# The join between a selective scan with FFN and a mixture-of-experts stage: who makes the last products, x2 and x3

## The reference

```
x1 = x  + tanh(g_xattn[0]) * channel_attention(layernorm(x), ctx)
x2 = x1 + tanh(g_ffn[0])   * ffn(layernorm(x1))
x3 = x2 + tanh(g_xattn[1]) * ssm(ctx, z=layernorm(x2))
out = x3 + tanh(g_ffn[1])  * moe(layernorm(x3))

def ffn(x):                       # ternary weights, groups of 64
    gate, up = split(x @ Wgu.T)   # hidden width 1024
    h = silu(gate) * up
    return rms_norm(h) @ Wp.T

def ssm(ctx, z):                  # 256 channels, 16 states each
    state = state * exp(delta * A) + (delta * u) * B     # along 256 positions
    y = sum over states(state * C) + D * u
    return y * silu(z)

def moe(x):                       # 64 experts, top 8, capacity 128
    probs = softmax(x @ router)
    out[token] += weight * expert(x[token])              # for the 8 chosen
```

## Time and profile before

| | |
|---|---|
| median of three runs | 451.32 us |
| the runs | 449.02 to 453.57 us |
| the profiled execution | 454.34 us |
| its span | 452.6 us |
| busy: PE, DVE, POOL, ACT | 347.7, 323.4, 297.1, 240.5 us |
| mean granted clock of PE | 0.907 |
| transfers | 81.56 MB, mean 180 GB/s |

### The profile page before, as it was taken

How to read it: one execution, slowest core, us unless ns; L and a number is a source line. 1 busy time by engine, 2 the same in 40 slices (tenths; PEclk the granted TensorE clock), 3 DMA queues, 4 the chain that set the end, 5 groups by cost and what they waited for, 6 DMA issues and landing times.

```text
span 452.6 us, 6836 instructions
## 1 busy us (share of the span) xinstructions
PE 347.7 (77%) x1843; PEld 240.3 (53%) x1843; DVE 323.4 (71%) x748; ACT 240.5 (53%) x467; POOL 297.1 (66%) x231
## 2 busy tenths in 40 slices
PE   4838934689897999998990479888888888898860
PEld 2423722245453445454790367767766666776650
DVE  3999598889998998999969845544544444454454
ACT  0999968688897878894438013322332232232210
POOL 3200036698997998998614547888788888888750
PEclk9987875599999989999996569999999899999995
DMA  9910402569979998986002237988888888865557
GB/s 247 376 39 13 140 0 76 178 207 322 275 263 314 277 299 271 302 272 198 0 2 88 90 84 193 224 204 204 202 198 197 197 197 197 199 150 95 85 94 242
DMA packets 62809, 81.56 MB, mean 180 GB/s; under 512 B 6130, under 2 KB 42786, under 8 KB 62786
## 3 DMA queue, kind: packets, MB, share of 16 engines
q1 hardware_dynamic: 51632, 64.43, 45.1%
q0 software_dynamic: 9984, 16.78, 19.3%
q10 hardware_dynamic: 1170, 0.08, 0.3%
HBM read 70.13 MB, written 11.14 MB: 180 GB/s over the span
## 4 chain that ended last, share of the span: by engine, by line
POOL 28%; PE 22%; issue 15%; DVE 12%; ACT 11%; DMA 11%; SPq 0%; DVEq 0%; POOLq 0%
POOL sums L650 9%; POOL ssm L575 7%; POOL ssm L639 6%; DMA ssm<-routed,idx 5%; PE bank L1263 3%; PE bank L1105 3%; PE bank L1051 3%; POOL ffn L594 2%; DMA ssm<-bc_rows 2%; DVE ssm L1470 2%; PE bank L1078 2%; PE bank L1228 2%; PE bank L1241 2%; DMA du<-sums 2%; DVE bank L1465 1%
## 5 line engine op out<-in xcount | busy, mean ns | idle before, releaser
L650 POOL DMA_INDIRECT sums<-ssm,idx x48 | 79.1, 1648 | 19.3 <-issue 13.2
L1588 DVE COPY ssm<-bank 128x256 f32<-128x256 f32 x64 | 27.0, 422 | 79.9 <-PE bank L1228 79.8
L575 POOL TENSOR_TENSOR ssm<-ssm,bc_buf 128x1024 f32<-128x1024 f32 (+1 forms) x33 | 75.9, 2301 | 11.1 <-DMA bc_buf<-bc_rows 3.9
L639 POOL DMA_INDIRECT ssm<-routed,idx x64 | 66.1, 1032 | 25.1 <-issue 16.8
L1470 DVE TENSOR_TENSOR_SCAN ssm<-ssm,bank 128x512 f32<-128x512 f32 x64 | 78.1, 1221 | 5.6 <-issue 2.7
L1263 PE MATMUL bank<-arena,ssm 128*128 (+1 forms) x256 | 56.9, 347 | 2.4 <-DVE ssm L1680 1.8
L918 ACT ACTIVATE ssm<-bank 128x256 f32<-128x256 f32 x64 | 24.5, 383 | 60.8 <-PE bank L1241 59.8
L1051 PE MATMUL bank<-ssm,ident 128*128 128x512 f32 x98 | 49.7, 618 | 8.5 <-POOL ssm L575 6.2
L925 ACT ACTIVATE ssm<-bank 128x96 f32<-128x96 f32 x64 | 16.0, 250 | 71.5 <-PE bank L1263 71.5
L1105 PE MATMUL bank<-xs,wguT 128*128 128x512 bf16 x192 | 46.6, 395 | 7.3 <-POOL xs L561 5.4
L1247 PE MATMUL bank<-ssm,xin 128*128 128x256 bf16 x384 | 52.0, 274 | 0.1
(11 more groups left out here) (219 smaller groups left out, 684.9 us busy)
## 6 DMA issues: line engine op xcount, KB each, us to landing
bc_buf<-bc_rows SPq DMA_DIRECT2D x32, 512.0 KB, 4.4
ssm<-bc_rows SPq DMA_DIRECT2D x22, 512.0 KB, 5.4
arena<-in_L_ffn_gate_proj SPq DMA_DIRECT2D x32, 192.0 KB
arena<-in_L_ffn_up_proj SPq DMA_DIRECT2D x32, 192.0 KB
arena<-in_L_ffn_down_proj SPq DMA_DIRECT2D x32, 192.0 KB
B_last<-bc_rows SPq DMA_DIRECT2D x10, 512.0 KB, 5.4
sums<-zero_f SPq DMA_DIRECT2D x1, 2304.0 KB, 14.1
arena<-in_L_ffn_w_gate_up SPq DMA_DIRECT2D x1, 2048.0 KB, 11.5
```

The source lines that it names most:

```text
L575: pool.tensor_tensor(prod[:, a:b, :], hs[:, a:b, :], C_buf[:, a:b, :], ALU.mult).then_inc(s.prod_ok, 1)
L639: pool.indirect_dma_start(out=xe[:, k, :], out_offset=None, in_=routed, in_offset=bass.IndirectOffsetOnAxis(ap=idx2[:, k, 0:1], axis=0)).t ...
L650: pool.indirect_dma_start(out=sums, out_offset=bass.IndirectOffsetOnAxis(ap=idx2[:, k, 1:2], axis=0), in_=ye[:, k, :], in_offset=None, com ...
```

## The change

Seven edits, all in that stretch.

1. Unit 15's gated product: DVE makes `hidden(15)` behind scan 61, ahead of steps 62 and 63, no longer behind step 63.
2. The last products with C (steps 62 and 63) are one DVE instruction of 128 x 1024 ahead of `coefficient(0)`, no longer two of POOL. PE waits for it with a new semaphore, `last_ok`. POOL makes `add_square(14)` ahead of product 30.
3. PE: `project(15)` comes ahead of `sum_early(15)`, and PE waits for the last scan before it writes the router's mean into bank 6.
4. `keep_projection(1)` is left out: `x2(1)` reads the projection from banks 1 and 2. The logits of the two halves, which go to these banks, wait for `x2` instead.
5. ACT's order: `gate_z(0)`, `keep_y(3)`, `keep_x2(0)`, `gate_z(1)`, `keep_x2(1)`.
6. PE: `own_part` is left out. Both halves' `turn_x2` come first, then the logits of x2 and y2 and `turn_y` of the first half, then those of the second. `turn_y` only transposes y2 into the banks of `x3_of`.
7. DVE adds the turned y2 to x2 in SBUF: `x3(c)`, four instructions behind each `select`, and the statistics read that. ACT makes the routed rows from it, and its four copies of x3 are left out.

```diff
-            def product(q, first=0, steps=2):
+            def product(q):
...
+            add_square(UNITS - 2)
             product(PAIRS - 2)
-            add_square(UNITS - 2)
             add_square(UNITS - 1)
-            product(PAIRS - 1, 0, 1)
-            product(PAIRS - 1, 1, 1)
             rms(1)
...
-            keep_projection(1)
...
+            gate_z(0)
+            keep_y(3)
             keep_x2(0)
-            keep_y(3)
-            gate_z(0)
+            gate_z(1)
             keep_x2(1)
-            gate_z(1)
...
                 for j in range(4 * c, 4 * c + 4):
-                    act.wait_ge(s.x3_ps, j + 1)
-                    act.activation(xn[j], x3_of(j), ACT.Identity, bias=nmr[:, j:j + 1], scale=rstd[:, j:j + 1]).then_inc(s.xn_sb, 1)
-            for q, k in enumerate((5, 4, 0, 3)):
-                act.activation(x_res[:, 2 * q:2 * q + 2, :], bank[k][:, :].rearrange("p (j d) -> p j d", d=D), ACT.Copy).then_inc(s.x3_sb, 1)
+                    act.activation(xn[j], x_res[:, j, :], ACT.Identity, bias=nmr[:, j:j + 1], scale=rstd[:, j:j + 1]).then_inc(s.xn_sb, 1)
...
-                    sum_state(f, 2, s.prod_ok, 2 * f + 2)
-                    sum_state(f, 3, s.prod_ok, 2 * f + 3)
+                    sum_state(f, 2, s.last_ok, 1)
+                    sum_state(f, 3, s.last_ok, 1)
...
-                sum_early(f)
+                if f < UNITS - 1:
+                    sum_early(f)
...
             project(UNITS - 1)
+            sum_early(UNITS - 1)
             squares(1, bank[7])
+            pe.wait_ge(s.scan_ok, STEPS)
...
             def logits_of_x2(c):
 
-                pe.wait_ge(s.po_copy, 4)
+                pe.wait_ge(s.x2_sb, 6 + 2 * c)
...
-            def add_y(c):
-
+            def turn_y(c):
+
+                pe.wait_ge(s.x2_sb, NT)
+                pe.wait_ge(s.y_sb, 4)
                 for j in range(4 * c, 4 * c + 4):
                     for h in halves:
-                        ins = pe.matmul(x3_of(j)[:, h * P:h * P + P], u[:, h, j * P:j * P + P], ident[:, :], start=False, stop=h == 1, skip_group_check=True)
+                        ins = pe.transpose(x3_of(j)[:, h * P:h * P + P], u[:, h, j * P:j * P + P], ident[:, :])
                     ins.then_inc(s.x3_ps, 1)
 
             turn_x2(0)
-            own_part(0)
+            turn_x2(1)
             logits_of_x2(0)
-            turn_x2(1)
-            own_part(1)
+            logits_of_y(0)
+            turn_y(0)
             logits_of_x2(1)
-            logits_of_y(0)
             logits_of_y(1)
-            add_y(0)
-            add_y(1)
+            turn_y(1)
...
             for f in range(UNITS):
-                for k in range(4 * f, 4 * f + 4):
-                    state(k)
-                if f in ON_DVE:
+                state(4 * f)
+                state(4 * f + 1)
+                if f == UNITS - 1:
+                    hidden(f)
+                state(4 * f + 2)
+                state(4 * f + 3)
+                if f in ON_DVE and f < UNITS - 1:
                     hidden(f)
...
-                dve.wait_ge(s.po_copy, 2 * c + 2)
+                if c == 0:
+                    dve.wait_ge(s.po_copy, 2)
+                else:
+                    dve.wait_ge(s.proj_ok, UNITS)
...
-                    dve.scalar_tensor_tensor(out=x_res[:, j, :], in0=xn[j], scalar=coef[:, j:j + 1], in1=x_res[:, j, :], op0=ALU.mult, op1=ALU.add).then_inc(s.x2_sb, 1)
+                    dve.scalar_tensor_tensor(out=x_res[:, j, :], in0=xn[j] if c == 0 else bank[1 + j // 2 - 2][:, (j % 2) * D:(j % 2) * D + D], scalar=coef[:, j:j + 1], in1=x_res[:, j, :], op0=ALU.mult, op1=ALU.add).then_inc(s.x2_sb, 1)
...
+            dve.wait_ge(ld_C[1], 16 * (PAIRS // 2))
+            dve.wait_ge(s.scan_ok, STEPS)
+            dve.wait_ge(s.sum_ok, 3 * (UNITS - 1))
+            dve.tensor_tensor(prod[:, 2:4, :], hs[:, 2:4, :], C_buf[:, 2:4, :], ALU.mult).then_inc(s.last_ok, 1)
             coefficient(0, 1)
             x2(0)
...
+            def x3(c):
+
+                for j in range(4 * c, 4 * c + 4):
+                    dve.wait_ge(s.x3_ps, (j | 1) + 1)
+                    dve.tensor_tensor(x_res[:, j, :], x3_of(j), x_res[:, j, :], ALU.add).then_inc(s.x3_sb, 1)
+
             select(0)
-            half_statistics(4, 0, x3_of, s.x3_ps)
+            x3(0)
+            half_statistics(4, 0, s.x3_sb)
             select(1)
+            x3(1)
             shifts(0)
-            half_statistics(4, 1, x3_of, s.x3_ps)
+            half_statistics(4, 1, s.x3_sb)
```

More of the change, by code:

```diff
@@ L121, in __init__ @@
         self.pair_ok = sem("pair_ok")
+        self.last_ok = sem("last_ok")
         self.hsq_ok = sem("hsq_ok")
@@ L561, in _ @@
                 pool.tensor_tensor(xs[:, 2, kc, c], xnT[:, kc, c], xs[:, 1, kc, c], ALU.subtract).then_inc(s.xs_lo, 1)
-            def product(q, first=0, steps=2):
+            def product(q):
                 pool.wait_ge(ld_C[q % 2], 16 * (q // 2 + 1))
-                pool.wait_ge(s.scan_ok, 2 * q + first + steps)
-                a, b = 2 * (q % 2) + first, 2 * (q % 2) + first + steps
+                pool.wait_ge(s.scan_ok, 2 * q + 2)
+                a, b = 2 * (q % 2), 2 * (q % 2) + 2
                 f = q // 2
@@ L834, in keep_y, with keep_projection @@
                 act.activation(y_buf[:, p % 2, (p // 2) * 512:(p // 2) * 512 + 512], bank[3][:, :], ACT.Copy).then_inc(s.y_sb, 1)
-            def keep_projection(th):
+            def keep_projection():
                 for k in range(2):
-                    act.wait_ge(s.proj_ok, 8 * th + 8)
-                    act.activation(xw[:, 4 * th + 2 * k:4 * th + 2 * k + 2, 0:D], bank[1 + k][:, :].rearrange("p (a m) -> p a m", m=D), ACT.Copy).then_inc(s.po_copy, 1)
+                    act.wait_ge(s.proj_ok, 8)
+                    act.activation(xw[:, 2 * k:2 * k + 2, 0:D], bank[1 + k][:, :].rearrange("p (a m) -> p a m", m=D), ACT.Copy).then_inc(s.po_copy, 1)
             def square(f):
@@ L870, in _ @@
                 if f == 8:
-                    keep_projection(0)
-            keep_projection(1)
+                    keep_projection()
             def keep_x2(c):
@@ L1220, in _ @@
             pe.wait_ge(s.idx_step, 1)
-            pe.wait_ge(s.x3_sb, 4)
+            pe.wait_ge(s.x3_sb, NT)
             pe.sem_inc(s.m_hT_ps, 1)
@@ L1498, in x2, with half_statistics @@
                 for j in range(4 * c, 4 * c + 4):
-                    dve.scalar_tensor_tensor(out=x_res[:, j, :], in0=xn[j], scalar=coef[:, j:j + 1], in1=x_res[:, j, :], op0=ALU.mult, op1=ALU.add).then_inc(s.x2_sb, 1)
-            def half_statistics(n, c, source, ready):
+                    dve.scalar_tensor_tensor(out=x_res[:, j, :], in0=xn[j] if c == 0 else bank[1 + j // 2 - 2][:, (j % 2) * D:(j % 2) * D + D], scalar=coef[:, j:j + 1], in1=x_res[:, j, :], op0=ALU.mult, op1=ALU.add).then_inc(s.x2_sb, 1)
+            def half_statistics(n, c, ready):
                 for j in range(4 * c, 4 * c + 4):
-                    dve.wait_ge(ready, j + 1 if source is x2_of else (j | 1) + 1)
-                    dve.bn_stats(stats[:, j, :], source(j)).then_inc(s.ln_stats, 1)
+                    dve.wait_ge(ready, j + 1)
+                    dve.bn_stats(stats[:, j, :], x_res[:, j, :]).then_inc(s.ln_stats, 1)
                 for j in range(4 * c, 4 * c + 4):
@@ L1508, in half_statistics @@
                     dve.bn_aggr(mv[:, j, :], stats[:, j, :]).then_inc(s.ln_stats, 1)
-            def x2_of(j):
-                return x_res[:, j, :]
+            dve.wait_ge(ld_C[1], 16 * (PAIRS // 2))
+            dve.wait_ge(s.scan_ok, STEPS)
+            dve.wait_ge(s.sum_ok, 3 * (UNITS - 1))
+            dve.tensor_tensor(prod[:, 2:4, :], hs[:, 2:4, :], C_buf[:, 2:4, :], ALU.mult).then_inc(s.last_ok, 1)
             coefficient(0, 1)
@@ L1518, in _ @@
             dve.tensor_tensor(router_sb[:, :, :], router_sb[:, :, :], part(bank[6][:, 0:1], (0, 2), (1, E)), ALU.subtract).then_inc(s.coef_ok, 1)
-            half_statistics(3, 0, x2_of, s.x2_sb)
+            half_statistics(3, 0, s.x2_sb)
             coefficient(1, 3)
@@ L1522, in _ @@
             mean_over_deviation(3, 0)
-            half_statistics(3, 1, x2_of, s.x2_sb)
+            half_statistics(3, 1, s.x2_sb)
             dve.tensor_reduce(d_e[:, :], ident[:, :].rearrange("p (a b) -> p b a", b=GE), AX.X, ALU.add).then_inc(s.diag_ok, 1)
@@ L1636, in rows @@
                 dve.wait_ge(s.idx_step, 5 * a + 5)
-            dve.wait_ge(s.prod_ok, PAIRS + 1)
+            dve.wait_ge(s.prod_ok, PAIRS - 1)
             dve.wait_ge(s.c_ident, 8)
@@ L1720, in _ @@
             three_parts(1, 10 * ROUNDS - 3)
-            dve.wait_ge(s.x3_sb, 4)
+            dve.wait_ge(s.x3_sb, NT)
             for q in range(4):
```

## The result

Four runs of the changed kernel have a median of 456.58 us (455.15 to 459.0), four of the one before 450.17. The ratio is 1.011, with a 95% interval of 1.0065 to 1.0154. Timed again beside the last experiments, with eleven runs of it and 22 of the one before, the ratio is 1.0117 (1.0078 to 1.0155). So the change makes the kernel slower: by 5.0 us going by the ratio, by 6.4 going by the two medians, by 5.3 going by the larger set. 453.7 was forecast, 2.4 above before. Ratios here leave out the few executions that took markedly longer than the rest, such as one of e1's at 526.19 us.

The account below looks back on a forecast made before the run. Engines, not transfers, were taken to bound the stretch from the scans' end to the first gather. Select(0) sooner -1.8, clock +2.2, x3 on DVE +2.0 gave +2.4 us on a 451.32 median: 453.7, range 449.9 to 456.6.

Parts of the forecast that it names:

- The last scan and the gated product: At the scans' end on DVE: the gated product ahead of scan 62 makes the last scan end 1.11 us later.
- The first `nmr`: On DVE: 3.68 us from L1454 to the first one, so it lands at 220.93.
- The gap on PE: Between the two halves' transposes of x2: PE idle from 220.1 to 224.85, over 4.5 us, waiting for ACT's keep_x2(0).
- x3: After each select on DVE: four additions, 0.34 us each, 2.7 us for all eight (bounds 2.4 and 3.2).
- From `select(0)` to `pos`: On DVE, to the addition of bank 7 into pos: 10.5 us instead of 8.5.
- the sum without the clock's term: Whole stretch with PE's clock staying full: +0.2 us, 451.5; as a rival its chance was 0.21.
- the clock's term: PE's work behind the gap, partly at half speed: costs 1.7 to 2.5 us, taken as 2.2.
- how long the low clock lasts: On PE behind the gap: 3.4 to 5 us of the work runs at half speed.
- The fall: On PE: the new gap brings the clock from 2.4 to 1.2 GHz, as in two stretches taken as idle.
- The clock stays low over the whole PE part: Rival, PE behind the gap: half clock until logits_of_y(1) ends at 242.5; +8.2 us, 459.5; chance 0.07.
- a blocking of DVE and POOL: Rival at the scans' end: DVE's last product takes 3.25 us, 1.9 more; +4.3 us, 455.6; chance 0.06.
- the three chances: Whole kernel's time: within 1% (4.5 us) 0.88, slower by over 1% 0.10, faster by over 1% 0.02.

Follow-up runs that it names:

- e1: The changed kernel with ACT's old order (keep_x2(0), keep_y(3), gate_z(0), keep_x2(1), gate_z(1)); ratio to the kernel before 1.0032.
- e2: The changed kernel with 20 extra matmuls, result unread, on PE between the two halves' transposes of x2; ratio to the kernel before 1.0018.
- e4: The kernel before with only x3 moved to DVE: own_part left out, y2 only transposed, routed rows from SBUF; ratio 0.9973.
- e8: The changed kernel with 16 extra matmuls behind turn_x2(1); first gather 44.60 us behind the last scan, 45.61 in the changed kernel; whole time not compared.
- e3: The kernel before with only the scans' end changed: gated product early, last products on DVE, x2(1) from PSUM; ratio 0.997.
- e5: The kernel before with ACT's new order alone; ratio 1.0095.
- e9: The kernel before with the changed scans' end and PE reordered so own_part fills waits; ACT's order and x3 as before; ratio 0.9942.
- e10: The changed kernel as it is, timed once more; ratio to the kernel before 1.0117.

## Why the prediction was right and where it wasn't

**The steps that held.** The last scan and the gated product: from the start of scan 61 to the end of scan 63 were 5.37 us and are 6.47, 1.10 more (forecast 1.11). L1454: 3.08 us behind the last scan, forecast 3.27. The first `nmr`: 6.75, forecast 6.95. The gap on PE: 4.71 us, forecast over 4.5 (220.1 to 224.85). x3: 1.32 us a half from start to start, forecast 1.35. From `select(0)` to `pos` without the wait: 10.44, forecast 10.5. And with the clock held (e2) the stretch is 1.4 us shorter than before while the last scan ends 1.1 later: -0.3, where the sum without the clock's term had +0.2. The measured change is over twice the forecast +2.4, and what is above it comes from the clock's term.

**The step that failed: how long the low clock lasts.** I said "3.4 to 5 us of the work behind the gap runs at half speed, which costs 1.7 to 2.5 us", and took 2.2. It was 19 us, and by e2 it costs 7.4, not 2.2. The fall was forecast rightly, though one argument for it was misread: the stretches 58 to 62 and 239 to 243 are not idle times shorter than the gap, but the parts that I had cut out of idle times of 6.43 and 10.36 us. The length I took from two stretches in which PE was doing something else, matmuls of 256 and 512 columns in the attention and at the start of the scans. In the first of them the low clock doesn't even follow a gap:

```profile
46.00:48.00 2.00, 2.00 (x6) 0.91 (x5) 1.90 (x1) 2.00 (x6) 0.00 (x0) 0.88 0.64 188
48.00:50.00 2.00, 2.00 (x6) 1.53 (x6) 1.97 (x2) 2.00 (x4) 0.00 (x0) 0.50 0.97 300
```

PE is busy throughout, from 44 on, and the clock falls from 1.00 (44 to 46) to 0.50 all the same. Behind the gap of the changed kernel stand transposes and logits, which run at a full clock where it is there (e4 without `own_part`, 220 to 233; e8, 234 to 244) and did not bring it back in 19 us. e8 shows the difference with everything else equal. "PE is busy" was read as if all busy stretches were alike.

**The rival that took its place.** "The clock stays low over the whole PE part" had 0.07. Its mechanism is what happened, down to the wait of `select(1)` for `logits_of_y(1)`: forecast 17.6 us from the end of the gap to the logits' end, measured 17.1 (221.14 to 238.2). I had given it so little since no row showed a low clock under over 10 us of dense work. No row excluded it either.

**Why the range held: luck.** The median of 456.58 lies 0.02 us under the upper end of the range, 456.6. That end was drawn for a blocking of DVE and POOL (455.6) and the spread of the runs, not for what happened. The rival's price of +8.2 us would have led to 459.5. Reading its parts from the last scan on, the measured stretch is +6.1, with 1.1 for the later last scan 7.2. The time moved by 5.0 to 6.4. What is missing, 0.8 to 2.2 us, was not found: the expert loop's time differs by more than that between executions. Of the three chances, the 0.88 for a change within 1% was too high and the 0.10 for slower too low by the same cause; the ratio is 1.011, and the intervals reach a little below 1.01.

**Two DVE-POOL cases.** The collision that I gave 0.06 happens, in e1 (product 2.05 us) and e3 (POOL's square 2.24 us, and a clock fall from it), and in neither profiled execution of the changed kernel. It hangs on when C lands for product 30, which moves by a us or two against the scans. I had taken POOL's end at 214.2 as fixed. The rule of the Trainium skill (SBUF — State Buffer, "Who interferes with whom") that whichever of the two starts first holds the other off fits both: DVE waited in e1, POOL in e3.

Left open: why the expert loop takes 196 us in some executions and 200 in others, and with it the 0.8 to 2.2 us between the stretch and the whole.

## What to carry to other kernels

A wait of PE can cost more than its length through PE's clock: 2.85 us of waiting made `select(0)` 5.96 us later in e5. When an edit opens a gap on PE, ask what work stands behind the gap, and take the length of the low clock only from rows where that same work followed a fall; work that holds a clock need not bring it back. Before reordering for a shorter chain, look for useful matmuls that can stand in the gap: `own_part` looks like 3.5 us of PE's time to be saved, and kept where PE would wait (e9) it is part of the version with the lowest ratio.

## What the runs showed of the hardware

- Behind a gap of 4.71 us the granted clock was 0.50 for 19 us in which PE was busy for 18.86 (again 0.50 over 220 to 238 in e10). It was back at 1.00 in the course of the positions' bf16 matmuls of 64 columns (0.61 over 240 to 241, 1.00 over 241 to 242).
- Two waits of 0.79 and 1.73 us, with PE busy for 5.48 of 8 us, were followed by a fall as well (e1). In the kernel before the clock fell within 46 to 50 us with PE busy throughout. Two waits of 0.83 us, ahead of 221.65 and 225.33, were not followed by one before 233 (e4).
- Sixteen bf16 matmuls of 512 columns (e8), or the f32 ones of 256 columns of `own_part` (e5, at 1.00 by 236), were what PE did as the clock rose.
- The Trainium skill (TensorE: Matmul & The Clock Gate, "What's actually happening") speaks of a hardware block that sets the clock by how busy PE has been. The traces agree where the clock fell in a gap of PE. In this plain form they support neither the fall within 46 to 50 nor the missing rise: by the profile PE was busy for 99% of the 19 us at half clock. What brings the clock back, beyond the rows above, the runs here don't tell.
- A DVE instruction with two SBUF inputs and a POOL instruction that reads SBUF held each other off in either direction, by 0.8 us (the DVE product, e1) and 1.0 us (POOL's square, e3).
